# LayerNorm adapter on one Trainium2 core: the mean of two batches made by ScalarE ahead of the second square, in place of VectorE

## What is computed

```python
h = relu(x @ W1[id] + b1[id])            # 128x512 @ 512x128
a = x + h @ W2[id] + b2[id]              # 128x128 @ 128x512
mean = jnp.mean(a, axis=-1, keepdims=True)
var = jnp.mean(jnp.square(a - mean), axis=-1, keepdims=True)
out = x + (a - mean) * lax.rsqrt(var + 1e-5) * gamma[id] + beta[id]
```

## Time and profile before

| | |
|---|---|
| median of 3 runs | 338.56 us (336.55 to 339.12) |
| the profiled execution | 336.89 us, its span 335.1 us |
| TensorE busy | 307.8 us, 92% of the span |
| VectorE busy | 315.9 us, 94% |
| ScalarE busy | 283.2 us, 85% |
| GpSimd busy | 258.5 us, 77% |
| granted TensorE clock | 0.991 of full speed on the average |

### The profile page before, as it was taken

How to read it: one execution, slowest core, us unless ns; L and a number is a source line. 1 busy time by engine, 2 the same in 40 slices (tenths; PEclk the granted TensorE clock), 3 DMA queues, 4 the chain that set the end, 5 groups by cost and what they waited for, 6 DMA issues and landing times. The chain is left out here.

```text
span 335.1 us, 8885 instructions
## 1 busy us (share of the span) xinstructions
PE 307.8 (92%) x2133; PEld 266.6 (80%) x2166; DVE 315.9 (94%) x668; ACT 283.2 (85%) x847; POOL 258.5 (77%) x298
## 2 busy tenths in 40 slices
PE   1696999999999999999999999999999999988960
PEld 0165989889889898898988888898898988877840
DVE  3495799999999999999999999999999999999996
ACT  6474899999999889999988998999999999887961
POOL 2023698888888889888888888988888888887882
PEclk9999999999999999999999999999999999999996
DMA  7999547666677666766667666666667766665333
GB/s 179 279 387 417 219 171 239 223 227 217 229 253 237 204 226 215 252 225 220 222 217 254 214 232 220 218 226 229 227 214 240 252 222 233 221 208 189 128 126 125
DMA packets 43077, 75.71 MB, mean 226 GB/s; under 512 B 3612, under 2 KB 8823, under 8 KB 42901
## 3 DMA queue, kind: packets, MB, share of 16 engines
q1 hardware_dynamic: 41733, 75.14, 66.3%
q10 hardware_dynamic: 1296, 0.01, 0.2%
HBM read 41.49 MB, written 33.55 MB: 224 GB/s over the span
## 5 line engine op out<-in xcount | busy, mean ns | idle before, releaser
L270 POOL TENSOR_TENSOR x_io<-x_io,beta_all 128x512 f32<-128x512 f32 x128 | 163.9, 1281 | 4.6 <-DVE ps_y L491 2.7
L386 PE MATMUL ps_h<-w_all,x_T 128*128 x1024 | 135.5, 275 | 0.1
L386 PEld LDWEIGHTS ps_h<-w_all,x_T 128*128 128x128 f32 x1024 | 124.4, 192 | 0.4 <-issue 0.3
L261 POOL TENSOR_TENSOR h_low<-h_T,h_high 128x128 fp32r<-128x128 f32 x128 | 60.6, 473 | 65.2 <-ACT h_T L334 53.5
L339 ACT ACTIVATE cut<-ps_y,row_sum 128x512 bf16<-128x512 f32 x128 | 90.1, 704 | 7.5 <-DVE ps_y L491 5.5
L516 DVE SCALAR_TENSOR_TENSOR x_io<-ps_y,rstd,x_io 128x512 f32<-128x512 f32 x128 | 94.7, 741 | 0.0
L508 DVE SCALAR_TENSOR_TENSOR ps_y<-ps_y,mean,gamma_all 128x512 f32<-128x512 f32 x128 | 89.9, 747 | 1.0
L379 PE MATMUL ps_T<-identity,x_io 128*128 128x128 f32 x512 | 77.2, 274 | 6.5 <-DMA x_io<-in_x 6.3
L319 ACT COPY x_T<-ps_T 128x512 f32<-128x512 f32 x128 | 76.8, 600 | 0.1
L405 PE MATMUL ps_y<-w_high,h_high 128*128 x128 | 68.9, 539 | 6.7 <-DVE w_low L480 2.9
L491 DVE SCALAR_TENSOR_TENSOR ps_y<-ps_y,x_io 128x512 f32<-128x512 f32 x98 | 67.1, 685 | 4.9 <-PE ps_y L408 4.9
(11 more groups left out here) (39 smaller groups left out, 219.5 us busy)
## 6 DMA issues: line engine op xcount, KB each, us to landing
x_io<-in_x SPq DMA_DIRECT2D x64, 512.0 KB, 4.4
out<-x_io SPq DMA_DIRECT2D x63, 512.0 KB, 3.0
w_all<-in_L_cond_W SPq DMA_DIRECT2D x10, 512.0 KB, 6.8
b_all<-in_L_cond_b SPq DMA_DIRECT2D x1, 2560.0 KB, 17.5
out<-x_io SPq DMA_DIRECT2D x2, 256.0 KB, 2.1
parts<-cut SPq DMA_DIRECT2D x3, 30.0 KB, 3.3
rows<-in_L_cond_b SPq DMA_DIRECT2D x1, 20.0 KB
rows<-in_L_cond_gamma SPq DMA_DIRECT2D x1, 20.0 KB
```

The source lines that it names most:

```text
L261: nc.gpsimd.tensor_tensor(h_low[:, j % H_SLOTS, :], h_T[:, j % H_T_SLOTS, :], h_high[:, j % H_SLOTS, :].bitcast(F32), ALU.subtract).then_i ...
L270: nc.gpsimd.tensor_tensor(x_io[:, j, :], x_io[:, j, :], of_lang(beta_all, lang), ALU.add)\
L386: last = nc.tensor.matmul(ps_h[:, 0:A], x_T[:, j % 2, c, :], w1_all[:, bass.ds(lang, 1), c, :].rearrange("p o a -> p (o a)"), start=(c == ...
```

## The change

The function `means` moves from VectorE's block to ScalarE's. There it is an activation (`nc.scalar.mul`, in the program an identity activation with the immediate scale 1/512 and an immediate bias 0) on the same two numbers per partition, called in `norm_sums` in front of the odd batch's `square`. It waits for `y_ready` of the odd batch, as the square behind it does, and raises `mean_ready`, for which VectorE's `scale` waits as before. VectorE's call in `step` goes.

```diff
             def norm_sums(t, j):
+                if j % 2 == 1:
+                    means(t, j)
                 square(t, j)
                 if j % 2 == 1:
                     root(t, j)
...
+            def means(t, j):
+                act.wait_ge(y_ready, t + 1)
+                nc.scalar.mul(mean[:, j - 1:j + 1], row_sum[:, j - 1:j + 1], 1.0 / H).then_inc(mean_ready, 1)
...
-            def means(t, j):
-                dve.wait_ge(y_ready, t + 1)
-                nc.vector.tensor_scalar(mean[:, j - 1:j + 1], row_sum[:, j - 1:j + 1], 1.0 / H, None, ALU.mult)\
-                    .then_inc(mean_ready, 1)
...
-                if has_means and j % 2 == 1:
-                    means(t - 2, (j - 2) % UNROLL)
```

## The result

The kernel before took 338.51 us (median of 20 runs), the changed one 341.18 us (20 runs): ratio 1.0074, 95% interval 1.0049 to 1.0098. The forecast was 337.3 us, 0.4% faster; it became 0.7% slower. The time lies in the range, the direction is wrong.

A forecast was written before the change was run, and what follows sets the result against it. ScalarE's queue was taken to set the quick pairs' pace, VectorE the last 43 us. Terms +2.9, -1.1 and -3.0 summed to -1.2 us, scaled to 337.3 us; range 333.8 to 342.3, 8 in 10.

The forecast's parts named there:

- What bounds the middle: From 60 to 290 us: VectorE's fullness partly false; ScalarE's queue sets the quick pairs' pace at 4.50 us.
- ScalarE's ring: Stretch of copy_h, square, root, relu and next copy_h on ScalarE, claimed to have no slack in a quick pair.
- quick pairs: Two-batch steps where GpSimd adds b2 for one batch, so no matmul L403; 4.50 us, forecast to grow to about 4.6.
- Step 1: VectorE loses 64 means, each holding it about 0.64 us; nothing waits longer for the result.
- Step 2: ScalarE gets 64 activations of 128x2 between copy_h and the second square, each delaying that square by 0.11 us.
- D: Delay of the odd batch's square on ScalarE from the added mean: taken as 0.11 us, range 0.09 to 0.29.
- The rival that the mean blocks ScalarE: Between copy_h and second square of quick pairs: delay 0.20 us gives 342.3 us, 0.29 gives 345.4; chance 18%.
- Step 3, first term,: Steady stretch, 49 to 290 us: 26 quick pairs pay 0.11 us each, +2.9 us.
- step 3's second: Steady stretch: the square's idle waits on VectorE in four places go, -1.1 us.
- The other pairs: Two-batch steps that are not quick, 4.71 to 4.74 us, with 0.22 us spare on ScalarE; claimed to pay nothing.
- Step 4, the end,: From 290 us to the end: nine means off VectorE give 3.0 us back, bounds 1.5 and 6.3.
- Stores move forward by less than a microsecond, which nothing awaits.: Steady stretch: GpSimd's and SyncE's work is only released earlier, by less than a microsecond for stores; no cost counted.

The follow-up runs named there:

- e1: Kernel before, plus a spare ScalarE mean ahead of the odd batch's square, result unused; VectorE keeps the used mean: 339.1 us, ratio 1.0044.
- e7: Kernel before with ScalarE's register load moved from behind the root to between copy_x_T and copy_h: 336.3 us, ratio 0.9972.
- e9: Kernel before, mean still on VectorE, with VectorE's register loads ahead of the odd add_x and ScalarE's between copy_x_T and copy_h: 336.3 us, ratio 0.9938.
- e2: Kernel before without any mean on any engine; scale reads a mean buffer set to zero: 339.8 us, ratio 1.0042.
- e6: e3 with ScalarE's register load also moved, from behind the root to between copy_x_T and copy_h: 334.6 us, ratio 0.9878.
- e3: Changed kernel with VectorE's two register loads of language ids moved ahead of the odd step's add_x: 361.2 us, ratio 1.0696.
- e4: Changed kernel with ScalarE's mean moved behind the odd batch's square, ahead of the root: 337.4 us, ratio 0.9985.
- e5: e3 with SyncE's wait ahead of a pair's store one batch longer, so the store is issued later: 341.7 us, ratio 1.0106.
- e11: Kernel before with only VectorE's register loads moved ahead of the odd step's add_x: 336.9 us, ratio 0.9950.

## Why the prediction failed, step by step

- **What bounds the middle.** Right in that VectorE's share was false, and that ScalarE's ring has no slack in quick pairs (e1). The trace also held what I had not read: TensorE is nearly level with it (e7), so little could be gained there: the stretch from batch 8 to 116 takes 251.0 us before and 249.0 in e9.
- **Step 1, VectorE loses its means.** Right in the busy time: 22 us less between 60 and 290 us, and 63 of the 64 means before ended within 0.06 us of the end of a GpSimd instruction. "Nothing waits longer for the result" was right as well. Wrong was to go on with 0.64 us a mean as time set free: the register loads ran under it, 94 of 98.
- **Step 2, D.** Taken as 0.11 us, measured 0.11 from mean to square and 0.09 on the pair. The estimate of 0.095 us by the Trainium skill, "ScalarE: Activation LUTs", section "What ACT_TABLE_LOAD costs", was as good. The rival that the mean blocks ScalarE (D of 0.20 and more) fell, though its 342.3 us is nearer to the measured time than the forecast: quick pairs of 4.7 us, which it needs, are 4.64.
- **Step 3, first term,** 26 quick pairs pay D, +2.9 us: right in mechanism, and 2.3 us in size by e1's 0.09. In the changed kernel the quick pairs together take 3.6 us longer: they are 4.64 in place of 4.59 while the second pattern holds, 5.21 once and 4.79 to 4.83 three times.
- **The step that failed: what VectorE's relief brings.** Two terms stand on it. The first is step 3's second, -1.1 us: "The other pairs pay nothing: their 0.22 us wait is for the odd batch's sum, which VectorE, freed of 0.64 us a pair, delivers earlier". Up to 118 us this holds: the sum is ready 0.03 us ahead of copy_h, where it was ready 0.31 behind it (medians), and these pairs stay at 4.71. From there on it comes 0.35 us behind, no earlier, so D comes on top and they take 4.80 (medians). The 28 other pairs together take 0.6 us more in place of 1.1 less. I subtracted the mean's 0.64 us and did not ask what ran under it: VectorE's register loads. e2 shows it with the relief alone, 4.92 us in the other pairs.
- **Step 4, the end,** is the second such term, and the largest miss: -3.0 us (bounds 1.5 to 6.3), measured -0.8, outside its bounds. With both loads covered the same move gives -2.6 us (e9 against e6). How the shortfall is made up was not told apart: 1.3 us of issue time in front of the reciprocal (3 times) and 1.5 us in front of `add_x` stand between 290 and 333 us, but e2, whose loads are uncovered too and whose ScalarE makes no mean, ends in 42.3 us, so the uncovered loads alone don't explain it. These are single profiles, and the four others with the mean on VectorE have ends of 44.0 to 44.7 us.
- **"Stores move forward by less than a microsecond, which nothing awaits."** Nothing waited for them, but ScalarE's register load met them: in the changed kernel once (0.90 us, the quick pair of 5.21), in e3 in all 45 pairs.
- **Sum.** The quick pairs were +3.6 for +2.9, the others +0.6 for -1.1, the end -0.8 for -3.0, and the start, for which nothing was forecast, gave -0.6: together +2.8 in place of -1.2 (2.7 by the spans).
- **Advice to offload.** The Trainium skill, "Perfetto Trace Analysis", section "Optimizing Scalar/DVE Operations", says that if VectorE is saturated, offloading some work to ScalarE may make sense. Here the 94% were partly a wait, and the move made the kernel slower. With both loads covered (e6 against e9) moving the mean gained 0.6%.

## What to carry to other kernels

Time in which an instruction is held (here a mean of two numbers that waits for GpSimd) can be cover for what stands behind it in the engine's queue; before you take such an instruction away, list the register loads, waits and DMA issues behind it and ask where they will lie. In this kernel it paid to put the register loads of VectorE and ScalarE ahead of an instruction that waits anyway (e6, e9), and to put a small operation where ScalarE waits for an accumulator (e4). Where one engine gets earlier, look at what it triggers: here SyncE's issue came to lie ahead of ScalarE's load by the distance at which it is slow, and an edit worth 0.5% in one kernel cost the other 6%. And before comparing medians that differ by under 1%, compare the granted clocks of the executions behind them.

## What the runs showed of the hardware

- **A register load is slow beside a DMA issue.** In the kernel before, between 60 and 290 us, all 169 register loads (line 139; ScalarE, VectorE, GpSimd, TensorE) that began 0.7 to 1.9 us after SyncE began to issue a pair's store took 0.47 to 0.94 us, and all 341 that began less than 0.6 or over 2.3 us after it took 0.27 to 0.32. In the changed kernel it is 129 of 130 over 0.45 us and none of 319. e3, e5 and e6 show that the distance matters for the time. Whether it is SyncE's issue or the transfers that it starts was not told apart.
- **A short activation.** 128x2 with an immediate bias lasts 0.20 to 0.21 us and holds the next activation back by 0.11; between a square and its root it holds back nothing.
- **An early drop of the clock.** In six of the 14 profiles, before and changed among them, TensorE's granted clock is 1.00 all through the first 60 us, and copy_h of batch 8 stands at 39.2 to 40.1 us. In the eight others it is at 0.5, the lower of its two levels (1.2 GHz), for 3.4 us (six profiles) or for 6.8 to 6.9 us (e6, e11) between 28.9 and 36.2 us, and that copy_h stands at 41.2 to 41.9 and at 42.6 and 42.3 us.

The same stretch in e6 and then in the kernel before, 20 matmuls in 5.87 busy us against 41 in 5.92:

```profile
29.40:36.20 6.80, 5.87 (x20) 5.21 (x22) 0.76 (x3) 2.16 (x6) 1.68 (x2) 0.50 1.08 439
```

```profile
29.40:36.20 6.80, 5.92 (x41) 5.40 (x43) 1.90 (x6) 4.26 (x13) 3.31 (x4) 1.00 1.05 425
```

From 20 to 28.9 us TensorE is busy 6.6 to 7.5 us in both kinds, so that does not tell why the clock falls in some. The delay is as large as the effect of the change, so spans of single profiles don't rank these kernels; lengths from batch 8 on can be compared.
